# A weight-combining stage shares one pair's PSUM eviction out differently, with two loads in another order

## The reference, cut to what matters

```python
B, N, T, O, G = 32, 256, 256, 256, 8
masked_w = weight * mask[None, :, :]              # weight (G,O,T), mask (O,T)
w_bot = jnp.einsum('bg,got->bot', y, masked_w)    # y = cond_8 (B,G): one weight matrix per sample
x = x + (jnp.einsum('bnt,bot->bno', x, w_bot) + bias)
```

## Time and profile before

| | us |
|---|---|
| median of 3 runs | 67.15 (67.11 to 68.97) |
| the profiled execution, whole | 67.48 |
| its span in the trace | 65.7 |
| TensorE busy | 60.1 (91% of the span) |
| VectorE, ScalarE, GpSimd busy | 47.6, 47.8, 6.0 |

### The profile page before, as it was taken

One profiled execution on the slowest core, in us unless ns is written; L12 is line 12 of the kernel. 1 busy time (PEld: TensorE's weight loads), 2 busy tenths in 40 slices (PEclk: granted clock), 3 DMA queues, 4 the chain that ended last, 5 costly groups with the idle time before them and its releaser, 6 DMA issues.

```text
span 65.7 us, 1490 instructions
## 1 busy us (share of the span) xinstructions
PE 60.1 (91%) x645; PEld 55.7 (85%) x645; DVE 47.6 (72%) x34; ACT 47.8 (73%) x40; POOL 6.0 (9%) x15
## 2 busy tenths in 40 slices
PE   2999579999999999999999999999999999999910
PEld 1269477977888899999999999999999999999900
DVE  2107919997866989999999999988999992250200
ACT  2400378699789999999999799999879976005520
POOL 5501752620000000000000000000000000000000
PEclk9999999999999999999999999999999999999998
DMA  0799999999995036954999999999999239907393
GB/s 0 257 423 352 387 418 410 438 414 414 434 419 220 25 40 279 417 225 185 242 299 205 412 437 422 399 444 414 399 427 409 115 135 402 399 27 324 157 372 109
DMA packets 5333, 20.20 MB, mean 308 GB/s; under 512 B 592, under 2 KB 1104, under 8 KB 4432
## 3 DMA queue, kind: packets, MB, share of 16 engines
q1 hardware_dynamic: 5040, 19.89, 78.1%
q10 hardware_dynamic: 288, 0.23, 1.2%
HBM read 11.73 MB, written 8.39 MB: 306 GB/s over the span
## 4 chain that ended last, share of the span: by engine, by line
PE 88%; ACT 5%; issue 1%; DVE 0%
PE slots L405 20%; PE slots L406 20%; PE slots L407 20%; PE slots L425 11%; PE slots L305 11%; ACT w_raw L498 5%; PE slots L414 4%; PE slots L299 3%; ACT weights L528 1%; DVE zeros L536 0%
## 5 line engine op out<-in xcount | busy, mean ns | idle before, releaser
L405 PE MATMUL slots<-x_hi,w_hi 128*128 128x256 f32 x112 | 31.5, 281 | 0.0
L407 PE MATMUL slots<-x_hi,w_lo 128*128 128x256 f32 x112 | 31.3, 279 | 0.0
L406 PE MATMUL slots<-x_lo,w_hi 128*128 128x256 f32 x112 | 31.3, 279 | 0.0
L406 PEld LDWEIGHTS slots<-x_lo,w_hi 128*128 128x128 f32 x112 | 21.1, 188 | 0.0
L405 PEld LDWEIGHTS slots<-x_hi,w_hi 128*128 128x128 f32 x112 | 21.1, 188 | 0.0
L407 PEld LDWEIGHTS slots<-x_hi,w_lo 128*128 128x128 f32 x112 | 21.1, 188 | 0.0
L550 DVE TENSOR_TENSOR x_lo<-x_ring,x_hi 128x2048 fp32r<-128x2048 f32 (+1 forms) x8 | 16.1, 2018 | 1.6 <-ACT x_hi L464 1.6
L464 ACT CAST x_hi<-x_ring 128x2048 fp32r<-128x2048 f32 (+1 forms) x8 | 13.4, 1692 | 1.5 <-DMA x_ring<-in_x 1.2
L482 ACT ACTIVATE weights<-slots,smalls 128x1024 f32<-128x1024 f32 x10 | 10.8, 1111 | 4.9 <-PE slots L407 4.9
L559 DVE TENSOR_TENSOR w_lo<-w_raw,w_hi 128x2048 fp32r<-128x2048 f32 x6 | 13.7, 2284 | 0.2 <-ACT w_hi L470 0.2
L498 ACT COPY w_raw<-slots 128x1024 f32<-128x1024 f32 x8 | 8.0, 1013 | 6.7 <-PE slots L305 6.6
(11 more groups left out here) (22 smaller groups left out, 15.6 us busy)
## 6 DMA issues: line engine op xcount, KB each, us to landing
out<-weights SPq DMA_DIRECT2D x15, 512.0 KB, 4.6
x_ring<-in_x SPq DMA_DIRECT2D x7, 1024.0 KB, 9.6
x_ring<-in_first SPq DMA_DIRECT2D x6, 512.0 KB, 6.3
weights<-in_first SPq DMA_DIRECT2D x4, 256.0 KB, 5.5
out<-weights SPq DMA_DIRECT2D x1, 256.0 KB, 2.4
out<-weights SPq DMA_DIRECT2D x1, 128.0 KB, 2.3
out<-weights ACTq DMA_DIRECT2D x1, 128.0 KB, 2.1
smalls<-in_small ACTq DMA_DIRECT2D x1, 97.0 KB, 3.1
```

Of the source, the lines that this page charges most:

```text
L405: nc.tensor.matmul(dst, wh, xh, start=(k == 0), stop=False)
L406: nc.tensor.matmul(dst, wh, xl, start=False, stop=False)
L407: last = nc.tensor.matmul(dst, wl, xh, start=False, stop=(k == KC - 1))
```

## The change

Unit 1's other part is no longer moved by VectorE. ScalarE copies it out of PSUM unmasked, as its first work, and GpSimd then multiplies the mask into `w_raw` in place, in four pieces of 8 samples (a new semaphore, `raw_masked`): piece 0 behind pair 1's masking, piece 1 behind pair 2's, pieces 2 and 3 behind pair 3's and behind `w_lo_ready` at 2. In exchange VectorE copies unit 1's diagonal part (a `tensor_copy`), and ScalarE doesn't. The count of `raw_by_act` at which a slot is free stays as it was, with unit 1's other part now the first to be counted.

The PSUM slots are numbered anew (`unit_slot`, `product`, `early`), so that units 2 and 4 put their diagonal part where unit 1's other part and unit 2's diagonal part were. Unit 7's identity matmuls now wait for `early_by_act` (ScalarE's move of the early result) and its other part for `raw_by_dve`.

Pair 3's two loads are issued ahead of the first half of group 0's x. Behind unit 7, `high_piece(2)` and `low_piece(2)` go ahead of the two halves of `high_x(1)` and `low_x(1)`. Reads of `w_raw` wait for `raw_masked` where they need it.

```diff
-ORDER = (..., ("masked", 2), ("other", 2), ("x", 0), ("masked", 3), ("other", 3), ("x", 1))
+MB = 8
+ORDER = (..., ("masked", 2), ("other", 2), ("masked", 3), ("other", 3), ("x", 0), ("x", 1))
...
         def product(g, h):
-            return slots[:, (2, 0, 3, 1)[(2 * g + h) % SLOTS], :]
+            return slots[:, (1, 0, 3, 2)[(2 * g + h) % SLOTS], :]
         def unit_slot(u, side):
+            if u < SIDES:
+                return slots[:, 2 * u + side, :]
             if u < EARLY:
-                return slots[:, 2 * (u % 2) + side, :]
-            return slots[:, ((0, 2), (3, 1))[u % 2][side], :]
-        early = slots[:, 1, 0:BANK]
+                return slots[:, ((0, 3), (1, 2))[u % 2][side], :]
+            return slots[:, ((0, 1), (3, 2))[u % 2][side], :]
+        early = slots[:, 3, 0:BANK]
...
             load_pair(2)
+            load_pair(3)
             load_half(0).then_inc(half_x_loaded, 16)
-            load_pair(3)
             load_half(1).then_inc(x_loaded[0], 16)
...
+            behind_pair = (None, (0,), (1,), (2, 3))
             for j in range(1, PAIRS):
                 pool.wait_ge(masked_loaded[j], 16)
                 for i in range(2):
                     nc.gpsimd.tensor_tensor(blocks[:, 2 * j, half_of(i)], ...)
+                if j == 1:
+                    pool.wait_ge(smalls_loaded, 16)
+                    pool.wait_ge(raw_by_act, 1)
+                if j == PAIRS - 1:
+                    pool.wait_ge(w_lo_ready, 2)
+                for i in behind_pair[j]:
+                    some = raw_columns(1, False)[:, i * MB:(i + 1) * MB, :]
+                    nc.gpsimd.tensor_tensor(some, some, smalls[:, AT_MASKS + SPAN:AT_MASKS + 2 * SPAN].unsqueeze(1).broadcast_to(
+                        [P, MB, SPAN]), ALU.mult).then_inc(raw_masked, 1)
...
                 else:
-                    pe.wait_ge(raw_by_dve, u - 1)
+                    pe.wait_ge(early_by_act, 1)
                 identity(u, on)
                 identity(u, on + 1)
-                if u <= EARLY:
-                    pe.wait_ge(raw_by_dve, u - 1)
-                else:
-                    pe.wait_ge(early_by_act, 1)
+                pe.wait_ge(raw_by_dve, u - 1)
...
             pe.wait_ge(raw_by_dve, UNITS // HO)
+            pe.wait_ge(raw_masked, 1)
             pe.wait_ge(half_x_loaded, 16)
             multiply_first(early, 0, 0, NB // 2).then_inc(early_ready, 1)
...
             def high_weights(g):
+                act.wait_ge(raw_masked, NB * g // MB + 1)
...
+            act.wait_ge(others_ready, 2)
+            nc.scalar.copy(raw_slot(1, False), made(1, False)).then_inc(raw_by_act, 1)
             for u in range(UNITS):
+                if u == 1:
+                    continue
                 if u == EARLY:
                     act.wait_ge(raw_by_act, UNITS // HO)
                     act.wait_ge(raw_by_dve, UNITS // HO)
+                    act.wait_ge(raw_masked, 1)
...
+            high_piece(2)
             for lo in (0, NB // 2):
                 high_x(1, lo, lo + NB // 2)
-            high_piece(2)
...
+                if u == 1:
+                    dve.wait_ge(diagonal_ready, u + 1)
+                    nc.vector.tensor_copy(raw_slot(u, True), made(u, True)).then_inc(raw_by_dve, 1)
+                    continue
                 dve.wait_ge(others_ready, u + 1)
...
+            low_piece(2)
             for lo in (0, NB // 2):
                 low_x(1, lo, lo + NB // 2)
-            low_piece(2)
```

More of the change, by code:

```diff
@@ L40 @@
 WARM = 5
-ORDER = (("other", 0), ("masked", 0), ("masked", 1), ("other", 1), ("off", 0), ("masked", 2), ("other", 2), ("x", 0),
-         ("masked", 3), ("other", 3), ("x", 1))
+ORDER = (("other", 0), ("masked", 0), ("masked", 1), ("other", 1), ("off", 0), ("masked", 2), ("other", 2),
+         ("masked", 3), ("other", 3), ("x", 0), ("x", 1))
 COLUMNS = {"masked": SLOT, "other": BANK, "off": (UNITS - SIDES) * SPAN, "x": WIDE // 2}
@@ L138, in conditional_residual @@
         raw_by_dve = sem("raw_by_dve")
+        raw_masked = sem("raw_masked")
         half_x_loaded = sem("half_x_loaded")
@@ L157, in conditional_residual, with raw_columns, raw_slot, made @@
         block = ctx.enter_context(nc.Block())
-        def raw_slot(u, diagonal):
+        def raw_columns(u, diagonal):
             half = u * SPAN // P
             at = (half if diagonal else 1 - half) * O + u * SPAN
-            return w_raw[:, :, at:at + SPAN].rearrange("p b (m r) -> p m b r", r=RT)
+            return w_raw[:, :, at:at + SPAN]
+        def raw_slot(u, diagonal):
+            return raw_columns(u, diagonal).rearrange("p b (m r) -> p m b r", r=RT)
+        def made(u, diagonal):
+            return unit_slot(u, diagonal_side(u) if diagonal else 1 - diagonal_side(u)).rearrange("p (m b r) -> p m b r", b=B, r=RT)
         pieces = ((0, NB // 2, 0), (NB // 2, NB, 0), (0, NB, 1))
@@ L497, in _ @@
                 act.wait_ge(diagonal_ready, u + 1)
-                nc.scalar.copy(raw_slot(u, True),
-                               unit_slot(u, diagonal_side(u)).rearrange("p (m b r) -> p m b r", b=B, r=RT)).then_inc(raw_by_act, 1)
+                nc.scalar.copy(raw_slot(u, True), made(u, True)).then_inc(raw_by_act, 1)
             act.wait_ge(raw_by_act, UNITS)
             act.wait_ge(raw_by_dve, UNITS)
+            high_piece(2)
             for lo in (0, NB // 2):
                 high_x(1, lo, lo + NB // 2)
-            high_piece(2)
             high_weights(2)
@@ L586, in _ @@
                     low_piece(1)
+                if u == 1:
+                    dve.wait_ge(diagonal_ready, u + 1)
+                    nc.vector.tensor_copy(raw_slot(u, True), made(u, True)).then_inc(raw_by_dve, 1)
+                    continue
                 dve.wait_ge(others_ready, u + 1)
-                nc.vector.tensor_tensor(raw_slot(u, False),
-                                        unit_slot(u, 1 - diagonal_side(u)).rearrange("p (m b r) -> p m b r", b=B, r=RT),
+                nc.vector.tensor_tensor(raw_slot(u, False), made(u, False),
                                         mask_off_of(u).unsqueeze(2).broadcast_to([P, PER * QU, B, RT]),
                                         ALU.mult).then_inc(raw_by_dve, 1)
+            low_piece(2)
             for lo in (0, NB // 2):
                 low_x(1, lo, lo + NB // 2)
-            low_piece(2)
             low_weights(2)
```

## The result

The changed kernel takes 68.22 us (median of 6 runs, 67.77 to 69.83), the kernel before 67.25 beside it; the ratio is 1.017 (1.012 to 1.022). So it is slower by about 1.5%, or 1 us. The forecast was 67.6 with a range up to 67.9: the sign and the load that TensorE waits for came out, the size was half of what was measured. Every ratio here is taken over the runs within 1.5% of the fastest of their kernel, where times and medians are of all runs.

What follows compares the result with a forecast made beforehand. TensorE bounds the kernel, busy 60.1 of 65.7 us. The removed wait's 1.08 us is lost to x landing at 14.1, so the early multiply comes 0.45 to 0.5 later than 13.61: 67.15 becomes 67.6, range 66.1 to 67.9.

Steps and rivals of the forecast that it cites:

- The sum: Early multiply at 14.1 + 0.05 against 13.61, so all behind it 0.45 to 0.5 us later; from median 67.15 to 67.6.
- The removed wait: TensorE's 1.10 us idle at 7.53 for unit 2's PSUM slot goes, so unit 2 starts 1.08 us earlier.
- The copies and GpSimd: VectorE's new copy takes 1.22 us, a GpSimd piece 0.73 (0.4 to 1.5); the piece costs nothing.
- The load that moves: First half of group 0's x, behind pair 3, lands at 12.7 to 12.8, or 14.1 when delayed by an instruction fetch.
- The link between the packet and late loads: An instruction fetch on one DMA engine makes the load under way behind it about 1.4 us late.
- The link between the packet and TensorE's progress: The fetch goes with TensorE's progress, 1.37 us after unit 4's start, so it moves from 12.4 to 11.35.
- From the early multiply on: The 4.32 us from the early multiply to the last 24 float32 matmuls of group 0 stay.
- the hand-over: Before group 1, piece 2 goes first: 3.3 us of copies within 4.27, 1.0 to spare, nothing gained or lost.
- The first (no strike): Rival, chance 0.38: the fetch doesn't delay x; early multiply at 12.80, 0.8 us earlier, time 66.35 (66.1 at best).
- The second, the lower clock: Rival, chance 0.05: TensorE's 1.6 us idle before the early multiply lowers its clock; at least 1.5 us more, about 69.1.
- The third (GpSimd): Rival, chance 0.05: GpSimd's in-place pieces take over 1.9 us and delay pairs 2 and 3; 67.7, or 67.2 with x in time.

Runs made afterwards that it cites:

- e6: Changed kernel with five matmuls on zeros added ahead of TensorE's wait for the first half of x: 67.89 us, ratio 1.013 to the kernel before.
- e7: Changed kernel as it is, timed and profiled once more beside the kernel before: 67.94 us against 67.04, ratio 1.014.
- e3: Changed kernel with nine matmuls on zeros added ahead of TensorE's wait for the first half of x: 68.05 us against 66.94, ratio 1.021.
- e11: Kernel before, unchanged, run for a second profile: 66.75 us, early multiply at 12.88.
- e1: Changed kernel with only the load order undone (first half of group 0's x ahead of pair 3 again): 66.70 us against 66.94, ratio 0.996.
- e8: Kernel of e1 with each of GpSimd's four masking pieces cut from 8 samples to one: ratio 0.996 to the kernel before.
- e4: Kernel before with 30 small matmuls added to TensorE's opening; packet moved from 12.4 to 9.8. Repeated as another run: ratio 1.004, median 67.58 against 67.40.
- e5: Kernel before with pair 3's loads ahead of the first half of x and 14 small matmuls in TensorE's opening: 68.57 us against 67.04, ratio 1.026.
- e2: Kernel before with only the load order changed (pair 3 ahead of the first half of x): median 67.77 us against 66.94, ratio 1.005.
- e14: Kernel of e1 with pair 1's two loads in the other order (masked weights last): 67.42 us against 67.09, ratio 1.006.

## Why the prediction was wrong in size, and where it was right

**The sum is the step that failed.** "Early multiply at 14.1 + 0.05 against 13.61: 0.5 later", and then 0.45 to 0.5 on top of the median of 67.15. The 14.1 is a landing time and doesn't get later when TensorE's opening is slow: x landed at 14.1 and 13.9 where the first pair ended at 6.7 (after, e6), at 13.8 and 13.6 where it ended at 7.1 and 7.2 (e7, e3). The 13.61 is the end of TensorE's own chain, in a run whose opening was slow. What a time has over the start of its early multiply is the same in both kernels: 67.48 - 13.61 = 53.87, 66.75 - 12.88 = 53.87 (e11), 67.75 - 13.93 = 53.82 (e7). By this, as an estimate, the medians of the kernel before (67.09 for all runs, 67.25 beside the changed kernel) stand for early multiplies at 13.2 to 13.4, and those of the changed kernel (67.94, 68.22) for 14.1 to 14.4. The difference is 0.9 to 1.0 and not 0.5. Carried absolutely the working was near: 67.98 for the profiled execution stood in the text, and 67.94 and 68.22 were measured. Setting it against the 67.15 would have given 0.8. It was the step to the median, which took 67.48 - 67.15 off the changed kernel as well, that put it at 67.6. The 417 ns were in the trace to be read.

**The removed wait.** It is right that it goes (unit 2's identities at 6.51, right behind the first pair; in e1 and e7 they wait 0.2 or less for ScalarE's new first copy). It is wrong that this is worth 1.08. Where the first pair ends at 6.7 to 6.8, unit 2 could go on at once, and it waits for pair 1's loads instead, until 7.28 in the first profile after and 7.83 in e1; in e7 it is 8.07. I had checked pair 1's masked weights against a start at 7.55 and never asked when its other load lands: 2.11 + 5.1 = 7.2. What is left is 0.3 us (e1). This error didn't enter the forecast, where x's landing decides.

**The copies and GpSimd.** Both were right: 1.22 for VectorE's copy (I took 1.22), 0.64 for a piece (0.73), and nothing of it on the path that the ratio of e8 could show.

**The load that moves.** The steps came out: x last of the same set, undisturbed, at 12.65 (12.7 to 12.8 forecast), and struck by the instruction packet at 14.1 (14.1 forecast) in the first profile. That the 14.1 fits so well is in part luck: the packet came at 10.9 and not at 11.35 (which is 1.4 ahead of 12.75, where 12.4 was 1.6 ahead of 14.0, so not quite "as far" as I wrote), in e7 x landed at 13.8, and there the loads were late before any packet. What stands last in a full queue comes late by whatever came late before it. The link between the packet and late loads, which rested on a single case, is shown by e4. The link between the packet and TensorE's progress is shown only in part (e5).

**From the early multiply on, and the hand-over.** Right: 4.29 against 4.32, 5.45 for the 24 matmuls, no idle in the second stage. The new order of piece 2 costs nothing that shows there; no run tried it alone.

**The rivals.** The first (no strike) is what e2's profile shows for x, but not the changed kernel. The second, the lower clock, came in 2 of 12 runs: in the one with a profile 3.2 us at 0.50, behind an idle of 2.17, and 5.93 us instead of 4.29 from the early multiply to the 24 matmuls, near its price. Given 0.05, it was rather too small. The third (GpSimd) fell with e8. The Trainium skill (Runtime: NRT & Kernel Launch, Instruction fetch mechanics) calls the cost of crossing into a block of instructions mostly hidden. No stop of TensorE like e5's shows in the changed kernel's profiles, so that is borne out there; but e4 shows the packet making other loads late by 1.2, and e5 a stop of 1.12 us that may be of this kind.

**What stays open.** Whether the long idle causes the low clock, what exactly TensorE waited for in e5, by what rule the packet moves, and how x's lateness in e7 divides between the packet and what was late before it. That earlier lateness comes with the new sharing more often than without: pair 1's masked weights landed at 6.9 or after, not at 6.3 to 6.5, in six of seven profiles with it, e14 with its own order aside, and in one of eight with the old. Whether the sharing causes it wasn't tried.

## What to carry to other kernels

When a transfer bound by the queue meets a chain bound by an engine, compare them as absolute times, and place the chain where the median run has it, not where the profiled run has it. Look at the opening for signs of how the profiled run stands (one shape of matmul with two durations), and hold its time against all runs. A wait for a slot that goes is worth only the distance to the next thing that lands: list every load of the unit behind it. And don't put the load that the critical multiply waits for last in a saturated queue: in five of the eight profiles here where x stood last, it landed 0.9 to 1.5 us later than in the other three.

## What the runs showed that I had not expected

30 small matmuls in TensorE's opening moved an instruction packet from 12.4 to 9.8 us and made each load behind it 1.2 us late; 14 of them didn't move it. But the 14, with the other order of loads, gave a stop of 1.12 us for which the profile names no cause (e5, 2.6% slower than before). TensorE's opening matmuls take 417 or 270 ns each, and how many take the longer time changes from run to run: the end of the first pair moves by 0.7 us, with the granted clock at 1.00 in both.
